# A log-step scan on one core: part of the weighted products made by ScalarE, and longer partial score sums on VectorE

## The reference, cut to what matters

```python
def _combine(left, right, W):
    B, T, C = left.shape
    hd = C // LANES                       # 4 lanes of 32 channels
    q = left.reshape(B, T, LANES, hd)
    k = right.reshape(B, T, LANES, hd)
    v = ((left + right) @ W).reshape(B, T, LANES, hd)
    scores = jnp.einsum('btld,btmd->btlm', q, k) * hd ** (-0.5)
    att = jax.nn.softmax(scores, axis=-1)
    z = jnp.einsum('btlm,btmd->btld', att, v)
    denom = (1.0 + jnp.arange(LANES, dtype=z.dtype))[None, None, :, None]
    z = _rms_norm(z) / denom
    return left + z.reshape(B, T, C)
```

## Time and profile before

| | us |
|---|---|
| median of 3 runs | 1735.6 (1734.5 to 1736.95) |
| profiled execution | 1737.16, its span 1735.4 |
| the scan, about | 1080 to 1590 |
| TensorE busy over the span | 1547.9 (89%) |
| VectorE busy | 1358.0 (78%) |
| ScalarE busy | 957.1 (55%) |
| GpSimd busy | 645.8 (37%) |

### The profile page before, as it was taken

How to read it: one execution, slowest core, us unless ns; L and a number is a source line. 1 busy time by engine, 2 the same in 40 slices (tenths; PEclk the granted TensorE clock), 3 DMA queues, 4 the chain that set the end, 5 groups by cost and what they waited for, 6 DMA issues and landing times. The chain is left out here.

```text
span 1735.4 us, 37728 instructions
## 1 busy us (share of the span) xinstructions
PE 1547.9 (89%) x13802; PEld 1017.8 (59%) x13802; DVE 1358.0 (78%) x2469; ACT 957.1 (55%) x2389; POOL 645.8 (37%) x592
## 2 busy tenths in 40 slices
PE   5699999999999999999984957999999999996486
PEld 3333333333333333333364856999999999996475
DVE  6789999999999999999553434698888888886633
ACT  4268888888888888888821324344444444442121
POOL 5300000000000000000034422888888888882634
PEclk9789999999999999999966987999999999998688
DMA  3320000000000000000073021011111222112520
GB/s 114 111 71 19 26 27 27 19 23 27 27 26 16 25 27 27 27 15 27 8 203 95 24 73 49 14 49 48 49 48 48 49 48 48 44 40 66 176 74 24
DMA packets 88407, 84.94 MB, mean 49 GB/s; under 512 B 12556, under 2 KB 74121, under 8 KB 88272
## 3 DMA queue, kind: packets, MB, share of 16 engines
q1 hardware_dynamic: 84176, 75.00, 15.5%
q0 software_dynamic: 4096, 8.13, 1.3%
HBM read 36.78 MB, written 23.59 MB: 35 GB/s over the span
## 5 line engine op out<-in xcount | busy, mean ns | idle before, releaser
L653 DVE TENSOR_REDUCE chunk_max<-ps_max 128x1 f32<-128x512 f32 (+3 forms) x1280 | 695.0, 604 | 72.4 <-PE ps_max L757 49.8
L707 ACT ACTIVATE probs<-ps_s 128x512 f32<-128x512 f32 (+3 forms) x1280 | 602.1, 533 | 152.6 <-PE ps_s L749 128.6
L1338 POOL TENSOR_TENSOR lane_products<-L,q 128x1024 f32<-128x1024 f32 x176 | 411.7, 2373 | 124.7 <-DMA L<-ident_rows 70.0
L740 PE MATMUL ps_max<-Ks,Qs 48*128 48x512 bf16 (+3 forms) x1280 | 378.9, 358 | 10.4 <-DMA Ks<-k_parts 9.6
L730 PE MATMUL ps_s<-Qs,Ks 50*128 50x512 bf16 (+3 forms) x1280 | 368.5, 350 | 11.0 <-DVE chunk_max L653 5.4
L804 PE MATMUL ps_o<-probs,Vp 128*32 128x512 f32 (+3 forms) x2560 | 340.8, 558 | 3.1 <-ACT O_sb L684 0.4
L730 PEld LDWEIGHTS ps_s<-Qs,Ks 50*128 50x128 bf16 x1280 | 111.8, 93 | 352.8 <-DVE chunk_max L653 321.7
L599 POOL TENSOR_TENSOR neg_max_b<-neg_max,no_max 128x8 bf16<-128x8 f32 x64 | 12.8, 200 | 515.2 <-DVE neg_max L638 515.2
L1644 DVE TENSOR_TENSOR weighted<-exp_scores,psV_s 128x2048 f32<-128x2048 f32 x88 | 197.0, 2280 | 0.0
L1735 PE MATMUL psZT<-ident,weighted 128*128 128x128 f32 x1408 | 167.3, 274 | 1.8 <-DVE weighted L1644 1.8
L1735 PEld LDWEIGHTS psZT<-ident,weighted 128*128 128x128 f32 x1408 | 158.1, 142 | 2.0 <-DVE weighted L1644 2.0
(11 more groups left out here) (234 smaller groups left out, 2263.4 us busy)
## 6 DMA issues: line engine op xcount, KB each, us to landing
m_w<-in_L_ffn_w_dram SPq DMA_DIRECT2D x24, 512.0 KB, 7.0
L<-q SPq DMA_DIRECT2D x16, 448.0 KB
Qs<-q_parts SPq DMA_DIRECT2D x192, 32.0 KB
Ks<-k_parts SPq DMA_DIRECT2D x192, 32.0 KB
dispatched<-blank SPq DMA_DIRECT2D x32, 132.0 KB, 2.4
L<-q SPq DMA_DIRECT2D x20, 192.0 KB
m_d<-dispatched SPq DMA_DIRECT2D x14, 264.0 KB, 4.7
L<-q SPq DMA_DIRECT2D x28, 128.0 KB
```

Source lines behind the costliest of these rows:

```text
L653: nc.vector.tensor_reduce(out, scores[:, 0:w], axis=AX.X, op=ALU.max).then_inc(max_reduced, 1)
L707: nc.scalar.activation(dst, ps_s[(k + r) % R][:, q0:], ACT.Exp, scale=SCALE).then_inc(exp_done, 1)
L740: last = nc.tensor.matmul(ps_max[(k + r) % R][:, 0:w], Q[r][rows, i * P:(i + 1) * P], K[r][rows, ck * QW:ck * QW + w], start=True, stop=no ...
L1338: return nc.gpsimd.tensor_tensor(c.lane_products[ch % 2][:, l].rearrange("p (j m) d -> p j m d", m=LANES), c.L[ch][:, :, l * W_LANE:(l + 1 ...
```

## The change: what it does

- PART goes from 8 to 12: VectorE reduces 12 product columns of each score, TensorE adds 20 instead of 24.
- The last 6 of the 32 rows of weighted products (OWN = 6, rows 26 to 31) are made by ScalarE. VectorE's second instruction makes 10 rows (16 to 25) instead of 16.
- After the exponentials ScalarE copies the last 192 columns of `psV` to `own_values` in SBUF (`own_copied`). VectorE's second instruction waits for that too, because its semaphore is what lets TensorE write `psV` anew.
- One section later ScalarE makes the 6 x 4 products, each an activation of 128 x 32 with `scale` set to a per-partition column of `expd`: 16 of them (EARLY = 4 rows) at the head of the section, ahead of the score copy, and 8 between the score copy and the exponentials (`own_weighed`).
- `expd` gets a second buffer, so that the old exponentials stay for that section.
- TensorE waits for `own_weighed` before the last 8 sums of z.

```diff
--- before.py
+++ after.py
@@ -1533,7 +1533,9 @@
     ROWS = CW * LA
     HC = CW // 2
     LAG = 3
-    PART = 8
+    PART = 12
+    OWN, EARLY = 6, 4
+    SHARED = ROWS - OWN
     with ExitStack() as cx:
         def sb(name, shape, dt=fp32):
             return cx.enter_context(nc.sbuf_tensor(name, shape, dt))
@@ -1551,7 +1553,8 @@
         part_scores = sb("part_scores", [P, LA * ROWS])
         best = sb("best_score", [P, LA * CW])
         shifted = sb("shifted_scores", [P, LA * CW, LA])
-        expd = sb("exp_scores", [P, LA, ROWS])
+        expd = [sb(f"exp_scores{u}", [P, LA, ROWS]) for u in range(2)]
+        own_values = [sb(f"own_values{u}", [P, OWN, LW]) for u in range(2)]
         total = sb("total", [P, LA, CW])
         mean_sq, log_ms, rs = (sb(n, [P, CW, LA]) for n in ("mean_sq", "log_ms", "rs"))
         psV, psZT, psZ = (ps(n, CE) for n in ("psV_s", "psZT", "psZ"))
@@ -1563,6 +1566,7 @@
         best_done, shifted_done, exp_done, total_done, weighed = (
             sem(n) for n in ("best_done", "shifted_done", "exp_done", "total_done", "weighed"))
         u_in_psum, uT_copied, v_in_psum = (sem(n) for n in ("u_in_psum", "uT_copied", "v_in_psum"))
+        own_copied, own_weighed = sem("own_copied"), sem("own_weighed")
         zT_in_psum, zT_copied, z_in_psum, z_done = (
             sem(n) for n in ("zT_in_psum", "zT_copied", "z_in_psum", "z_done"))
         squared, ms_done, rs_log, rs_done = (sem(n) for n in ("squared", "ms_done", "rs_log", "rs_done"))
@@ -1635,18 +1639,20 @@
                                             ALU.subtract).then_inc(shifted_done, 1)
                     dve.wait_ge(exp_done, g)
                     nc.vector.tensor_reduce(total[:].rearrange("p l j -> p (l j)"),
-                                            expd[:].rearrange("p l (j m) -> p (l j) m", m=LA), axis=AX.X, op=ALU.add)\
+                                            expd[v][:].rearrange("p l (j m) -> p (l j) m", m=LA), axis=AX.X, op=ALU.add)\
                       .then_inc(total_done, 1)
                     wait(dve, zT_in_psum, (g - 2) * 2)
-                    for half in range(2):
-                        rows = slice(half * ROWS // 2, (half + 1) * ROWS // 2)
+                    for half, rows in enumerate((slice(0, ROWS // 2), slice(ROWS // 2, SHARED))):
+                        count = rows.stop - rows.start
                         dve.wait_ge(v_in_psum, (g - 1) * 2 + (half + 1))
+                        if half:
+                            dve.wait_ge(own_copied, g)
                         nc.vector.tensor_tensor(weighted[v][:, rows],
-                                                expd[:, :, rows].rearrange("p l r -> p r l").unsqueeze(3)
-                                                .broadcast_to([P, ROWS // 2, LA, LW]),
-                                                psV[:, half * CE // 2:(half + 1) * CE // 2]
+                                                expd[v][:, :, rows].rearrange("p l r -> p r l").unsqueeze(3)
+                                                .broadcast_to([P, count, LA, LW]),
+                                                psV[:, rows.start * LW:rows.stop * LW]
                                                 .rearrange("p (r d) -> p r d", d=LW).unsqueeze(2)
-                                                .broadcast_to([P, ROWS // 2, LA, LW]), ALU.mult).then_inc(weighed, 1)
+                                                .broadcast_to([P, count, LA, LW]), ALU.mult).then_inc(weighed, 1)
                 if reached(g, 2):
                     dve.wait_ge(squared, g - 1)
                     wait(dve, rs_log, g - 2)
@@ -1667,18 +1673,35 @@
                     act.wait_ge(zT_in_psum, (g - 2) * 2 + (half + 1))
                     nc.scalar.activation(zT[:, cols], psZT[:, cols], ACT.Copy).then_inc(zT_copied, 1)
 
+                def weigh_own(places):
+                    for k in places:
+                        for l in range(LA):
+                            last = nc.scalar.activation(weighted[u][:, SHARED + k, l, :], own_values[u][:, k, :], ACT.Copy,
+                                                        scale=expd[u][:, l, SHARED + k:SHARED + k + 1])
+                    return last
+
                 def copy_u(half):
                     cols = slice(half * CE // 2, (half + 1) * CE // 2)
                     act.wait_ge(u_in_psum, g * 2 + (half + 1))
                     nc.scalar.activation(c.UT[u][:, cols], psU[:], ACT.Copy).then_inc(uT_copied, 1)
 
+                if reached(g, 2):
+                    act.wait_ge(own_copied, g - 1)
+                    wait(act, zT_in_psum, (g - 3) * 2)
+                    weigh_own(range(0, EARLY))
                 if reached(g, 1):
                     act.wait_ge(sT_in_psum, g)
                     nc.scalar.activation(scores_T[:], psS[:, 0:P], ACT.Copy).then_inc(sT_copied, 1)
+                if reached(g, 2):
+                    weigh_own(range(EARLY, OWN)).then_inc(own_weighed, 1)
+                if reached(g, 1):
                     act.wait_ge(shifted_done, g)
-                    wait(act, weighed, g * 2 - 2)
-                    nc.scalar.activation(expd[:].rearrange("p l r -> p (l r)"), shifted[:].rearrange("p r m -> p (r m)"),
+                    wait(act, weighed, g * 2 - 4)
+                    nc.scalar.activation(expd[v][:].rearrange("p l r -> p (l r)"), shifted[:].rearrange("p r m -> p (r m)"),
                                          ACT.Exp, scale=LW ** -0.5).then_inc(exp_done, 1)
+                    act.wait_ge(v_in_psum, g * 2)
+                    nc.scalar.activation(own_values[v][:].rearrange("p r d -> p (r d)"), psV[:, SHARED * LW:], ACT.Copy)\
+                      .then_inc(own_copied, 1)
                 if reached(g, 2):
                     copy_z(0)
                 if reached(g, 1):
@@ -1761,7 +1784,9 @@
                     turn_scores()
                 if reached(g, 2):
                     sum_z(range(HC // 2, HC))
-                    sum_z(range(HC, CW))
+                    sum_z(range(HC, SHARED // LA))
+                    pe.wait_ge(own_weighed, g - 1)
+                    sum_z(range(SHARED // LA, CW))
                 if head:
                     pe.wait_ge(c.l_loaded[ch], s * (16 * SHIFT_MOVES) + 16 * SHIFT_MOVES)
                     sum_u(0)
```

## The result

The changed kernel takes 1753.36 us, median of 4 runs (1752.21 to 1754.91), against 1736.15 for the kernel before measured beside it (1734.5 to 1736.95): a ratio of 1.0102, 95% interval 1.009 to 1.0114. It is 17.2 us slower; 24.4 were forecast. The profiled execution has a span of 1750.5 us.

The account below looks back on a forecast made before the run. TensorE's instruction count was taken as the bound, 11.10 us a section. 42 x 0.47 = 19.7, + 2.7 for the loop's turn, + 2.5 end, - 0.5 start made 24.4 us more: 1760.0 against the median 1735.6, range 1733 to 1779.

Parts of the forecast that it names:

- The bound before: In mid-scan TensorE's 98 instructions at 0.11 us plus one 0.18 us pause set the section, 11.10 us.
- The gain on TensorE, 0.45 us: Four of 24 transposing score sums go, saving 0.45 us per section; alone this would make a section 10.65 us.
- VectorE: Per section, partial sums cost 0.5 to 0.6 us more, products 0.80 to 0.84 less; VectorE stays below the bound.
- The price of a product: Each new ScalarE activation with a pointer takes 316 ns, one every 0.218 us; 24 take 5.2 us per section.
- The circle: Waits from one score copy to the next through ScalarE, TensorE and VectorE: 8.08 us, 11.57 with the 16 products.
- turn to sum of squares: From TensorE's turn of the scores to VectorE's sum of squares: 6.08 us, all paced by TensorE and unchanged.
- The loop's turn: ScalarE's jump back, no longer in a hole, costs 0.3 us nine times: 2.7 us, bounds 0 and 0.4 each.
- Start and end: Section 2's earlier score sums give -0.5 us; the last section's 24 activations and half-clock sums give +2.5 us.
- Sum: Whole kernel: 19.7 + 2.7 + 2.5 - 0.5 = 24.4 us slower.
- TensorE as the bound: Rival: below 0.189 us per activation the change gains, below 0.160 fully; 1717 us; chance 0.14.
- Double price: Rival: the pointer costs twice as much, 0.305 us per activation, section 13.4 us, 1835 us or more; chance 0.02.
- The clock: Rival: TensorE's 0.9 us pauses lower its clock in one section of four, adding some 40 us: 1800; chance 0.04.

Follow-up runs that it names:

- e3: The changed kernel with a constant scale instead of the per-partition pointer in ScalarE's 24 activations: 1718.24 us, ratio 0.9895.
- e9: The changed kernel with four ScalarE rows, 13 partial columns, products split 4 before the logarithm, 8 before and 4 after the score copy: 1730.58 us, ratio 0.9829.
- e2: The changed kernel with 8 partial columns again, so only ScalarE's 24 products remain of the change: 1756.4 us, ratio 1.012.
- e1: The kernel before with 12 instead of 8 partial columns and nothing moved to ScalarE: 1727.16 us, ratio 0.995.
- e10: The changed kernel, unaltered, measured once more beside later versions: 1776.62 us against 1759.08 for the kernel before, ratio 1.0096.
- e6: The changed kernel with 20 products ahead of the score copy and 4 behind it, instead of 16 and 8: 1809.99 us, ratio 1.0301.
- e4: The changed kernel with the first 4 of the 16 products moved before the logarithm of the section before: 1720.94 us, ratio 0.9915.
- e8: The changed kernel with four rows on ScalarE, 12 products ahead of the score copy and 4 behind, 13 partial columns: 1738.63 us, ratio 0.9887.

## Why the prediction was right, point by point

*The bound before.* Right. TensorE's count, with its one pause of 0.18 us, set the section: with ScalarE's circle out of the way (e3, e9) the section is just TensorE's 94 instructions (10.65) or 93 (10.54), 0.11 us apart.

*The gain on TensorE, 0.45 us.* Right in size (e2: the pause shrinks by 0.46) and right in being lost: it became part of TensorE's wait for the score copy, 0.74 us in the trace, 0.9 forecast. Wrong is the remark that it would alone make a section 10.65 us, if it means the longer sums alone: e1 has 10.87, because VectorE then sets the length.

*VectorE.* Partial sums 1.74 us, and the two product instructions 3.67 instead of 4.47 us, 0.80 less. Right. In the change VectorE doesn't bind, since it loses these rows. Its wait for the turned scores is 0.44 us, not the 0.6 given as a sign, and ScalarE is busy for 86 per cent of the time (342.40 of 396 us) rather than nine tenths.

*The price of a product.* 316 ns forecast, 308 measured; one every 0.218 us forecast, 0.2125 measured. By the figures in the Trainium skill ("ScalarE: Activation LUTs", section "What ACT_TABLE_LOAD costs") the estimate was one every 213 ns; the trace agrees, with 212.5. The rows moved cost ScalarE 24 x 0.2125 = 5.1 us a section and had cost VectorE 0.80.

*The circle.* Right in what closes it, and 0.19 us shorter than what I summed:

| link | forecast | measured |
|---|---|---|
| score copy to turn | 0.33 | 0.30 |
| turn to sum of squares | 6.08 | 5.99 |
| to the logarithm | 1.28 | 1.29 |
| to the inverse root, to the products | 0.39 | 0.40 |
| 16 products | 3.49 | 3.40 |
| sum | 11.57 | 11.38 |

Two terms were too large by 0.09 us each. One is the 16 products. The other is "turn to sum of squares", which the prediction called all paced by TensorE. In the section that it was read from, VectorE's own products ended last (1317.50 + 4.47 = 1321.97, with the sum of squares at 1321.89). ScalarE's squares, before and after:

```profile
1320.59 1.22 ACT L1697 ACTIVATE z_squares<-psZ 128x256 f32<-128x256 f32 x4 [0.28 <-PE psZ L1743]
...
1326.37 1.22 ACT L1720 ACTIVATE z_squares<-psZ 128x256 f32<-128x256 f32 x4 [0.28 <-PE psZ L1766]
```

The sum of squares started 0.08 us after they ended before, and 0.03 after they ended in the changed kernel. That is 0.05 of the 0.09. The other 0.04 lies between the turn and the squares' end (6.00 against 5.96 us): behind its pause TensorE's next weight load starts 0.06 us after the turn's (1321.63, 1321.69), before it was 0.10 (1315.81, 1315.91). In all the circle was taken 0.19 us too long, 42 x 0.19 = 8.0 us too much, which is more than the whole miss of 7.2; other terms were too small.

*The loop's turn.* 2.7 us forecast, too little. ScalarE where the loop jumps back:

```profile
1305.96 0.23 ACT L1731 ACTIVATE rs<-log_ms 128x32 f32<-128x32 f32 x1
1306.46 3.51 ACT L1679 ACTIVATE weighted<-own_values,exp_scores 128x32 f32<-128x32 f32 x16 [0.27 <-issue]
```

It takes 0.50 us from the inverse root to the products instead of 0.14. From score copy to score copy the section with the jump is 11.75 to 11.77 us and the one behind it 11.45, where the others have 11.37: 0.38 + 0.08 = 0.46 us, nine times, 4.1 us. What remains of 482.41 - 42 x 11.37 - 4.1, 0.8 us, is for the most part in the first three of the 42 sections (11.68, 11.50 and 11.45).

*Start and end.* The end: from section 44's score copy to the last inverse root 18.73 us against 16.26 before, +2.47 where I had 2.5; TensorE waits 2.50 us for the 24 products. That the size fits is partly luck. The sums of z end 13.74 us after that score copy instead of 11.85, so they are late by 1.9 us only: the last eight ran at 0.11 us each (0.86 us), not at the 0.16 that I took from the earlier trace rows. What follows took 0.6 us longer than before: TensorE's two groups of four weight loads for the turned z take 0.83 and 0.72 us against 0.47 and 0.42, at a granted clock of 0.59 (1598 to 1604 us) against 1.00 (1582 to 1587 us).

The start: section 2's score copy comes 1.34 us earlier instead of 0.5. The four score sums are worth 0.45 of it, near the 0.5 forecast; in both kernels they run at 0.11 us each. 0.09 lies ahead of the first score copy. The other 0.80 is the clock, here between the first two score copies, before and after (table of stretches):

```profile
1094.00:1104.00 10.00, 8.36 (x58) 8.12 (x59) 6.39 (x6) 1.97 (x8) 9.19 (x4) 0.83 0.01 2
...
1094.00:1104.00 10.00, 8.12 (x67) 7.46 (x68) 6.26 (x7) 6.61 (x30) 10.00 (x6) 1.00 0.01 2
```

Before, the weight loads of U's second half stand 0.21 us apart there (the lower level of 1.2 GHz), after the change 0.11. The change isn't what decides this: in e10, the same kernel once more, the granted clock is 0.83 between these copies and they lie 9.97 us apart, not 9.17. So 0.8 us of the difference between the two traces is luck of the executions.

*Sum.* -1.34 + 16.04 + 2.47 = 17.17 us up to the last inverse root (1604.02 against 1586.85), where 24.4 were forecast: 6.4 of the miss lie in the sections (22.4 forecast for them and the loop's turn) and 0.8 at the start. The span grew by only 15.1, so 2.1 us came back in the mixture of experts behind the scan. No run was made for that; as the medians are 17.2 apart, it may be that one execution.

*The rivals.* TensorE as the bound: not so. I gave 0.189 us per product as the point of no change and 0.160 as that of full gain; e3, at 0.12, gives the full gain. No run lies between 0.12 and 0.2125, so the two points themselves are not tested. Double price: not so, 0.2125 us and not 0.305. The clock: 1.00 in mid-scan with pauses of 0.74 us in every section, and 1.00 as well in e6 (1161 to 1557 us) with pauses of 1.60. The Trainium skill's kernel whose clock swings with short pauses ("TensorE: Matmul & The Clock Gate", section "A second HAM failure mode: psum-queue depth-cycling") has no counterpart in mid-scan here.

## What to carry to other kernels

A wait of an engine is not room for work if what ends the wait and what follows it lie on a circle through the other engines: add up the circle, with the new work in it, and compare it with the busiest engine's own length. Work may go into a wait up to that difference (e4, e9); beyond it each product costs its full time (e6). And when a change has two halves, run each alone: here one was worth 8.5 us and the other lost 21. The two don't add up, either: together they lose 17, because inside the closed circle the first half's gain is lost but for 3 us (e2).

## What the runs showed that I had not expected

ScalarE's jump back in this loop costs 0.36 us where no wait hides it (0.27 us of it shown as idle by issue), and it was enough to hold TensorE for 0.46 us once in four sections (e8). And two engines within 0.1 us of each other did not disturb each other here: in e9 a section takes TensorE's 10.54 us, while VectorE is busy for 95 per cent of the time (360.04 of 379 us) and, with its wait for the exponentials, would need about 10.48. This 10.48 is an estimate: e1's 10.87, plus 0.14 for the longer partial sum (1.88 against 1.74 us), less 0.53 for the shorter products (3.94 against 4.47).
